# Graph network on one core: casts of the adjacency moved to GpSimd, products of zeros ahead of the first weights, all orders written anew

## The reference, cut to what matters

```python
def gat(x, W, a_src, a_dst):                    # layers 0 and 1
    h = x @ W.T
    e = leaky_relu((h @ a_src)[:, :, None] + (h @ a_dst)[:, None, :], 0.2)
    return softmax(where(adj == 0, -big, e)) @ h

def layer2(x):                                  # adj in {0, 1}: only a0 is used
    e = leaky_relu((x * a0) @ x.T, 0.2)
    return sigmoid(where(adj == 1, e, -big)) @ x + bias2

def layer3(x):
    return (adj == 1) @ x @ W3[0] + bias3

x = layernorm(x + gat(x, W0, ...))
x = layernorm(x + gat(x, W1, ...))
x = layernorm(x + layer2(x))
x = layernorm(x + layer3(x))
```

## Time and profile before

| | |
|---|---|
| median of 3 runs | 272.94 us (271.94 to 273.21) |
| the profiled execution | 267.62 us |
| its span, first to last instruction | 265.8 us |
| instructions in the span | 6017 |
| DMA moved | 21.79 MB, mean 82 GB/s |
| granted TensorE clock, mean | 0.984 |

### The profile page before, as it was taken

One profiled execution on the slowest core, in us unless ns is written; L12 is line 12 of the kernel. 1 busy time (PEld: TensorE's weight loads), 2 busy tenths in 40 slices (PEclk: granted clock), 3 DMA queues, 4 the chain that ended last, 5 costly groups with the idle time before them and its releaser, 6 DMA issues.

```text
span 265.8 us, 6017 instructions
## 1 busy us (share of the span) xinstructions
PE 232.5 (87%) x1799; PEld 205.9 (77%) x1799; DVE 246.7 (93%) x956; ACT 217.7 (82%) x626; POOL 139.3 (52%) x161
## 2 busy tenths in 40 slices
PE   3878969899998999999999999999999969996850
PEld 3767758689877888889897889898999769786740
DVE  1799999999999989999999999999999999999883
ACT  1637526788999999899999999999999979987841
POOL 1001105312485483788766617554697556778851
PEclk9999999999999999999999999999999999999985
DMA  6787470000070005524000542103000110000033
GB/s 237 280 253 240 138 273 27 1 2 0 9 271 1 2 0 128 192 60 179 0 2 2 197 155 86 42 1 122 0 0 2 39 44 27 13 2 1 4 118 123
DMA packets 12147, 21.79 MB, mean 82 GB/s; under 512 B 1104, under 2 KB 5968, under 8 KB 12112
## 3 DMA queue, kind: packets, MB, share of 16 engines
q1 hardware_dynamic: 11680, 21.17, 23.8%
q10 hardware_dynamic: 432, 0.20, 0.3%
HBM read 17.17 MB, written 4.19 MB: 80 GB/s over the span
## 4 chain that ended last, share of the span: by engine, by line
DVE 50%; PE 26%; issue 9%; ACT 5%; POOL 5%; DMA 3%; DVEq 0%; POOLq 0%; ACTq 0%
PE banks L1123 11%; DVE wgt_all L808 11%; DVE fstats L856 9%; DVE fres L849 7%; DVE fres L841 5%; POOL frstd L542 4%; PE banks L1064 4%; DVE wgt_all L815 3%; PE banks L1089 3%; DVE raw_all L731 2%; PE banks L1120 2%; DMA adj_all<-adj_turned 2%; DVE top L783 2%; PE banks L1081 1%; PE banks L1100 1%
## 5 line engine op out<-in xcount | busy, mean ns | idle before, releaser
L542 POOL TENSOR_TENSOR frstd<-fvar,minus_half 128x4 f32<-128x4 f32 x64 | 73.7, 1157 | 102.0 <-DVE fvar L862 35.1
L1123 PE MATMUL banks<-vals_all,wgt_all 128*128 128x129 f32 x512 | 63.3, 277 | 3.5 <-DVE wgt_all L808 3.5
L1123 PEld LDWEIGHTS banks<-vals_all,wgt_all 128*128 128x128 f32 x512 | 59.6, 191 | 5.3 <-issue 3.1
L808 DVE SCALAR_TENSOR_TENSOR wgt_all<-banks,gain,maskT 128x256 f32<-128x256 f32 x128 | 52.5, 472 | 1.0 <-PE banks L1081 0.9
L538 POOL TENSOR_TENSOR xb<-xs_all,bias_cen 128x256 f32<-128x256 f32 x60 | 44.9, 772 | 8.6 <-DVE xs_all L765 4.4
L856 DVE BATCH_NORM_STATS2 fstats<-fres 128x6 f32<-128x256 f32 x128 | 47.6, 413 | 0.0
L1089 PE MATMUL banks<-fxT,fxTa 128*128 128x256 f32 x128 | 35.8, 382 | 0.0
L1123 PE MATMUL banks<-xs_all,wgt_all 128*128 128x128 f32 x256 | 31.6, 277 | 4.8 <-DVE wgt_all L815 4.7
L1123 PEld LDWEIGHTS banks<-xs_all,wgt_all 128*128 128x128 f32 x256 | 29.9, 192 | 5.4 <-issue 3.2
L640 ACT ACTIVATE xs_all<-fres,frstd 128x128 f32<-128x128 f32 x96 | 30.9, 427 | 2.0 <-POOL frstd L542 1.8
L637 ACT ACTIVATE xs_all<-fres,fcenter,frstd 128x128 f32<-128x128 f32 x64 | 26.5, 497 | 3.8 <-DVE fcenter L873 3.7
(11 more groups left out here) (93 smaller groups left out, 440.0 us busy)
## 6 DMA issues: line engine op xcount, KB each, us to landing
adj_all<-adj_turned SPq DMA_DIRECT2D x16, 512.0 KB, 4.8
xT_all<-x_turned SPq DMA_DIRECT2D x16, 256.0 KB, 4.4
x_all<-x_laid SPq DMA_DIRECT2D x16, 256.0 KB, 4.0
out<-xs_all SPq DMA_DIRECT2D x16, 256.0 KB, 2.3
bias<-biases_laid SPq DMA_DIRECT2D x1, 128.0 KB, 3.3
w_pack<-W_and_columns ACTq DMA_DIRECT2D x1, 68.0 KB, 2.7
w_fast<-W_turned ACTq DMA_DIRECT2D x1, 64.0 KB, 3.7
w_nat<-in_L_gnn_W ACTq DMA_DIRECT2D x1, 64.0 KB, 5.5
```

The costliest lines, as they stand in the source:

```text
L542: nc.gpsimd.tensor_tensor(frstd[:, int(l), slot(n), :], fvar[:, int(l), slot(n), :], minus_half[:, :, :], ALU.pow).then_inc(fast_pool[k], 1)
L808: last = nc.vector.scalar_tensor_tensor(out=wgt(u)[:, c, :], in0=place(f"rows{l}", u), scalar=gain[:, u, c, 1:2], in1=maskT(u)[:, c, :], o ...
L1123: last = nc.tensor.matmul(place(f"out{l}", u)[:, b * width:(b + 1) * width], wgt(u)[:, c, b * P:(b + 1) * P], (vals if l in "01" else xs)( ...
```

## The change

All 16 raw steps go from DVE to POOL, and 10 of the 16 mask steps (teams 2, 3, 5, 7, 8, 9, 10, 12, 13, 15) from ACT to POOL. SP's loads, PE's scores and DVE's seen now wait for whichever engine does raw. PE issues 9 products of the zero tile with itself ahead of the packed W0 product and 4 behind it. The rings keep their depths.

```diff
@@ sync
-                    sp.wait_ge(fast_dve[(n - ADJ) % K], at("dve", "raw", final(n - ADJ)))
+                    rawer = doer("raw", n - ADJ)
+                    sp.wait_ge(signals[rawer][(n - ADJ) % K], at(rawer, "raw", final(n - ADJ)))
@@ gpsimd
-            steps = {"bias": biases, "pow": powers, "low": low_part}
+            def make_raw(l, n, k):
+                pool.wait_ge(fast_adj_in[n % ADJ], loaded(n * H, ADJ))
+                for u in graphs(n):
+                    if n >= RAW:
+                        pool.wait_ge(fast_pe[(n - RAW) % K], at("pe", "score", u - RAW * H))
+                        pool.wait_ge(seen_step, SEEN.index(n - RAW) + 2)
+                    nc.gpsimd.tensor_scalar(raw(u), adj_in(u), -1.0, 1.0, ALU.mult, ALU.add).then_inc(fast_pool[k], 1)
+
+            def make_mask(l, n, k):
+                pool.wait_ge(fast_adj_in[n % ADJ], loaded(n * H, ADJ))
+                if n >= MASK:
+                    pool.wait_ge(fast_pe[(n - MASK) % K], at("pe", "agg", final(n - MASK)))
+                for u in graphs(n):
+                    nc.gpsimd.tensor_scalar(maskT(u)[:, :, :], adj_in(u), 1.0, 0.0, ALU.mult, ALU.add).then_inc(fast_pool[k], 1)
+
+            steps = {"raw": make_raw, "mask": make_mask, "bias": biases, "pow": powers, "low": low_part}
@@ vector, note_seen
-                dve.wait_ge(fast_dve[k], at("dve", "raw", final(n)))
+                rawer = doer("raw", n)
+                dve.wait_ge(signals[rawer][k], at(rawer, "raw", final(n)))
@@ tensor, scores
+                    rawer = doer("raw", n)
+                    pe.wait_ge(signals[rawer][k], at(rawer, "raw", u))
@@ tensor
+            def idle_products(count):
+                for _ in range(count):
+                    nc.tensor.matmul(banks[:, 5, 0:P], zero[:, :], zero[:, :], start=True, stop=True)
+
+            pe.wait_ge(zero_set, 1)
+            idle_products(9)
             projection_weights(0)
+            idle_products(4)
```

All five lists and the PSUM banks are written anew. Their first steps, before and after:

```diff
 sp
-  xT:0 adj:0 xT:1 xT:2 adj:2 adj:1 x:0 adj:3 xT:3 x:3 xT:4 adj:4 adj:6 ...
+  xT:0 xT:2 adj:0 xT:1 xT:3 adj:2 x:0 adj:1 adj:3 xT:5 x:2 adj:4 x:3 ...
 pe
-  h0:0 dT0:0 top0:0 h0:1 rows0:0 h0:2 dT0:1 out0:0 dT0:2 top0:1 ...
+  h0:0 h0:2 dT0:0 top0:0 dT0:2 h0:1 top0:2 rows0:0 h0:3 dT0:1 ...
 act
-  gains0:0 mask:0 vals0:0 mask:2 mask:1 gains0:1 mask:3 vals0:1 ...
+  mask:0 gains0:0 vals0:0 gains0:2 vals0:2 mask:1 gains0:1 vals0:1 ...
 dve
-  logits0:0 peak0:0 raw:0 dmax0:0 shift0:0 seen:0 logits0:1 weight0:0 raw:2 peak0:1 logits0:2 raw:1 ...
+  logits0:0 peak0:0 logits0:2 dmax0:0 shift0:0 peak0:2 seen:0 dmax0:2 shift0:2 logits0:1 weight0:0 peak0:1
+  logits0:3 weight0:2 seen:2 rsum0:0 peak0:3 dmax0:1 rinv0:0 shift0:1 res0:0 stats0:0 rsum0:2 dmax0:3 var0:0
+  rinv0:2 shift0:3 weight0:1 weight0:3 res0:2 logits1:0 ...
 pool
-  pow0:0 pow0:1 pow1:0 pow0:2 bias2:0 pow0:3 pow0:4 pow1:1 ...
+  raw:0 mask:2 raw:2 raw:1 mask:3 raw:4 pow0:0 raw:3 pow0:2 pow0:1 mask:5 raw:6 pow0:3 pow1:0 mask:7 bias2:0 ...
```

More of the change, by code:

```diff
@@ L461, in loaded @@
             return u // (depth * H) * 16 + 16
+        SEEN = [n for name, l, n in order("dve") if name == "seen"]
         signals = {"pe": fast_pe, "act": fast_act, "dve": fast_dve, "pool": fast_pool}
@@ L731, in make_raw @@
                     nc.vector.tensor_scalar(raw(u), adj_in(u)[:, :, :], -1.0, 1.0, ALU.mult, ALU.add).then_inc(fast_dve[k], 1)
-            SEEN = [n for name, l, n in order("dve") if name == "seen"]
             def note_seen(l, n, k):
-                dve.wait_ge(fast_dve[k], at("dve", "raw", final(n)))
+                rawer = doer("raw", n)
+                dve.wait_ge(signals[rawer][k], at(rawer, "raw", final(n)))
                 dve.wait_ge(seen_step, SEEN.index(n) + 1)
```

## The result

Over 20 runs the changed kernel takes 274.62 us in the median (270.52 to 279.17), beside 270.12 (268.56 to 273.91) for the kernel before in 20 runs on the same chip. The ratio is 1.0104, 95% interval [1.0063, 1.0145]: slower by 1.04% of 270.12, 2.8 us. The forecast was 5.3 us faster, and 264 to 271 us its own range. Executions more than 1.5% above the fastest of the same kernel are left out of all ratios (10 of the 20 of the changed kernel; the medians over all runs are 1.7% apart), and the profile of after is of such a one, 278.31 us, so I read busy times and places from it, never its span.

The account below looks back on a forecast made before the run. DVE's work plus its idle head and tail was taken to bound the span. Raw leaving -11.6, steps coming to DVE +3.3, locks +2, head +1 give -5.3: 272.94 to 267.6 us, own range 264 to 271, 8 in 10 261.5 to 276.

Parts of the forecast that it names:

- Raw leaves DVE: DVE: 32 casts, 12.4 us busy, go; two lie in the fill, so 11.6 us come off the path.
- New waits of POOL's queue: POOL, fill: pow0:0 stands behind 12 casts; mask:3 at 20.0 us, wanted at 21.8; cost 0.
- it remains the least full engine: POOL: 52 casts add 47 us, bringing it from 139 to some 182 us busy, ends 161 and 208.
- Locks: Between POOL and DVE: small two-input DVE instructions stand until a POOL instruction ends; +2 us, from -1 to +5.
- a cast at 0.62 us was cheaper than the 0.9 taken: POOL: a 512-element cast priced by the select at 0.9 us, ends 0.5 and 1.4.
- ACT's relief: ACT: loses 20 casts, 11.4 us, one norm team and 4 table loads, 5.1 us; priced at nothing for the span.
- The head: Start, PE: zero products delay h0:0 to 5.8 us, first weights at about 12.1; +1 us, from +0.3 to +2.2.
- SP's adj:2: SP's queue: adj:2, behind xT:3, issued at about 8 us instead of 2.64; just in time, cost 0.
- two page rules: POOL and DVE: shared ports shut each other out, 2 us; one-input work at best 769 ns for 512, or roughly line-rate.
- D: POOL, fill: casts above 1.1 us make mask:3 late for weight0:3; at 2 us a cast +4.7 us, 277.6; chance 0.18.
- Rival C: Middle stretch: PE's 141.84 of 146 us is its limit, later casts bring nothing; -1.3 us, 271.6, no change; chance 0.18.

Follow-up runs that it names:

- the casts alone: Kernel before, its orders and banks kept, no zeros, with all raws and the same ten masks moved to POOL where they ran in time: 1.0048.
- the early raws: Kernel before, its orders kept, no zeros, with only the raws of teams 0 to 6 moved to POOL: 1.001.
- the short masks: Kernel before, ACT's masks of teams 9, 10, 12, 13 and 15 converting 4 of each 256 columns: 1.0045; with DVE's late raws shortened too, 0.9966.
- 32 casts added: Kernel before, with POOL doing only the 32 spare casts of teams 7 and on, for which nobody waits: 1.0335, 9.1 us slower.
- 52 powers: Kernel before, with POOL doing 52 extra powers of 4 elements in place of the 52 spare casts: 1.0716, 19.4 us slower.
- short raws on DVE: Kernel before, DVE's raws of teams 7 to 15 converting only 4 of every 256 columns, nothing added: 0.9885, 3.1 us faster.
- the exchange rate measured at the same places: Kernel before, late raws on DVE and five late masks on ACT shortened, 32 late spare casts added on POOL: 1.024, 6.5 us slower.
- tiny casts: Kernel before, with the 52 spare casts on POOL cut to 4 elements instead of 512: 1.006, 1.6 us slower.

## Why the prediction was wrong

The steps that failed, as the prediction put them:

- **"Raw leaves DVE ... 11.6 us come off the path."** With the casts alone moved, DVE's busy time fell by 4.8 us and the span did not follow. The 14 early raws, called the surest gain, are worth nothing when POOL does them (1.001); the 18 late ones, nearly done away with, gave 3.1 us in one series and, together with the short masks, 0.9 in another, where 4.5 was expected. I had read 98% busy from 12 to 66 us as a bound, and added DVE's idle time and its work up to the span. But DVE's list is strict and its steps also wait for other engines: where the early raws went, DVE waits for PE instead (14.64 us busy from 12 to 30 us, 17.41 before).
- **"New waits of POOL's queue ... I cost it at 0"**, and before it "it remains the least full engine". This is the step that turned the sign: with the late casts made short the changed kernel is at 0.996 instead of 1.0104, so 3.9 of the 8.1 us between forecast and result are POOL's time with these casts. I looked at one power, pow0:0, in the fill; it did come in time (21.86 us, before 23.48), and so did the masks. I did not price the 32 casts of the later teams, most of them in the stretch in which POOL was busy 93 of 146 us already: 9.1 us when nothing is given in exchange (put into the kernel before as spare casts). POOL's share of the chain was 5%, and I took it for slack. A chain shows what was late in one execution, not what would be late with more work ahead of it: with 32 casts added the share is 18%, with 52 powers 29%.
- **"Locks ... I take +2 us."** Seen, and larger on DVE: its busy time is 251.7 us, or 248.0 without the zeros, instead of the 240 to 243 forecast. But the marks that I named, center and shift, did not rise, while norm did, and one alpha: the longest stop stands against POOL's adds and low parts, not against casts. In the casts alone, in the old orders, norm stays at 7.7 us, so its rise belongs to the new orders. Taking seven norms off DVE gave no time back, so this term was too small as busy time, and what it is worth in the span stays open.

What held, and what did not: a cast at 0.62 us was cheaper than the 0.9 taken; POOL's busy time is 166 instead of 182. ACT's relief was rightly priced at nothing: the short masks alone gave no gain. The head: nine zero products took 4.04 us instead of the 2.3 priced, since each is two instructions (and so were the 8 of the earlier trace rows, which are four products); so h0:0 began at 6.99 us instead of 5.8. But h0:0 and h0:2 then ran in 1.95 us, and the first weights came at 12.22, where 12.1 was forecast: that this fits is in part luck, for the errors cancelled. SP's adj:2 went out at 8.45 (about 8). The zeros are worth nothing in either direction. Of the two page rules weighed there, the one of the SBUF — State Buffer page (Trainium skill, the section on the two separate sides) is borne out in its direction: two-input DVE work stood behind POOL's, and once for six instructions in a row, not for one. In the GPSIMD Engine Reference (Trainium skill), 4.1 calls one-input work roughly line-rate; here a cast took POOL 620 ns and DVE 408 in the median, 1.5 times as long. The figure in 3.1 of that page, 769 ns for 512 elements at best, was too high here, and the measurement decides.

Of the rivals D came nearest: 4.7 us slower forecast, 2.8 measured, and slower because of POOL. Its trigger, casts above 1.1 us that make mask:3 late in the fill, never came; the load told in the full middle. Rival C, that PE takes over (271.6, no change), has its mechanism against it: PE is less busy in the middle than before, and short raws on DVE gave 3.1 us there.

What stays open: the really moved casts cost 0.5%, the exchange rate measured at the same places 2.4%. The really moved ones also take DVE's raw casts away in full, which in the kernel with 52 spare casts stood 3.3 us longer, they change who frees the adjacency slots, and the 14 early raws go along; which of these gives the 5 us back was not tried. Nor is it settled how the 1.4% that shorter casts give back to the changed kernel divides between lateness and lock: there the waits for POOL's powers sum to 5.2 us, hardly more than the 4.5 of before. No kernel here that does all of the work beats the one before; the nearest are the early raws and the zeros, at no difference.

## What to carry to other kernels

An engine at half its time is not spare if others wait in the full stretch for its small steps: before giving it work, list its latency-bound steps (here 64 powers of 1.01 us) and count who stands behind each of them. Spare work that nobody waits for, put into the kernel before, measures what more load costs; here it was from 1.6 / 10.2 = 0.16 (tiny casts) to 9.1 / (32 x 0.618) = 0.46 us (late casts) for each us of work, on an engine that was 52% busy. It was more than the real move cost, 0.5% in the old orders, so it warns and doesn't price. And a busy share near 100% says where relief can help, not that it will: shorten the work first, and read what comes off.

## What the runs showed of the hardware

- An int32 to bf16 cast with a multiply and an add on POOL takes 618 ns for 128x512 and 196 ns for 128x4: (618 - 196) / 508 = 0.83 ns an element, half of what the select's row had led me to the earlier trace rows. A power of 4 elements takes 1.01 us.
- A DVE instruction with two inputs (alpha, the larger of two tiles) stood once for 4.77 us through six POOL instructions in a row instead of slipping in between; its median is 683 ns. Norm, one input from SBUF with a scalar beside it, has a median of 283 ns and a longest of 831. These are DVE's rows at 249.80, where four norms take 1.71 us:

```profile
249.80 1.71 DVE L782 TENSOR_SCALAR xs_all<-fres,frstd 128x128 f32<-128x128 f32 x4
```

- The clock goes with part of the spread: before's profile has the lower level, 1.2 GHz, for its last 8.3 us alone, after's also in three earlier places (36.5 to 39.9, 87.7 to 91.1 and 231.0 to 234.5 us). Over the repeated runs of before in each series of the experiments, a run is 0.22 to 0.35 us longer for each us more at the lower level (by mean clock and span; correlation 0.83 to 0.97).
